# Decoder layers of a fused kernel: residual sums kept in PSUM, statistics of two blocks at once, the write-back moved, weights prepared in mid-slot

## The reference

```
x = x + attn(layernorm(x))          # 4 layers of width 128, hidden width 512
x = x + xattn(layernorm(x), ctx)    # channel selection by ctx (8 x 256 x 1024)
x = x + ffn(layernorm(x))           # top 2 of 8 experts, 1024 x 1024
```

```
h = x @ Win.T + bin
for each of 4 layers:
    y = silu(layernorm(h) )
    h = h + sconv(y) * scl              # decaying complex recurrence along the sequence
    y = silu(layernorm(h) @ W1.T + b1)
    h = h + y @ W2.T + b2
out = layernorm(h) @ Wout.T + bout

k = 154                                  # of 256 channels, for each of 1024 columns
mask = top_k(channel_map over channels, k)
```

## Time and profile before

| what | us |
|---|---|
| median of 3 runs (lowest, highest) | 1114.65 (1114.28, 1115.48) |
| the profiled execution: time, span | 1115.55, 1113.7 |
| busy over the span: PE, DVE, ACT, POOL | 1004.9, 555.0, 375.1, 447.8 |
| embedding and setup, until about | 99 |
| layer slots 0 to 16, until about | 371 |
| output product, mask applied, routing, until about | 592 |
| expert products, until about | 1101 |

### The profile page before, as it was taken

One profiled execution on the slowest core, in us unless ns is written; L12 is line 12 of the kernel. 1 busy time (PEld: TensorE's weight loads), 2 busy tenths in 40 slices (PEclk: granted clock), 3 DMA queues, 4 the chain that ended last, 5 costly groups with the idle time before them and its releaser, 6 DMA issues. The chain is left out here.

```text
span 1113.7 us, 13360 instructions
## 1 busy us (share of the span) xinstructions
PE 1004.9 (90%) x3534; PEld 531.0 (48%) x3535; DVE 555.0 (50%) x1660; ACT 375.1 (34%) x1016; POOL 447.8 (40%) x567
## 2 busy tenths in 40 slices
PE   5788889998998969799829999999999999999995
PEld 5687455564545435335514444444444444444442
DVE  5645779899997788978973111111111111111111
ACT  2334677786775328748820000000000000000000
POOL 3842455464653010008606433444333333333331
PEclk9878889999999989899958999999999999999998
DMA  7320111010000331003786473464637355373332
GB/s 300 119 92 3 49 49 38 30 67 1 1 1 1 152 114 39 1 1 155 296 322 232 89 227 79 128 182 129 176 76 229 77 138 163 75 226 75 75 76 38
DMA packets 38462, 120.25 MB, mean 108 GB/s; under 512 B 6220, under 2 KB 9351, under 8 KB 38408
## 3 DMA queue, kind: packets, MB, share of 16 engines
q1 hardware_dynamic: 25592, 79.77, 19.4%
q0 software_dynamic: 12816, 39.86, 16.4%
HBM read 82.91 MB, written 36.70 MB: 107 GB/s over the span
## 5 line engine op out<-in xcount | busy, mean ns | idle before, releaser
L2059 PE MATMUL bank<-T,X 128*128 x1184 | 508.4, 592 | 0.1
L2059 PEld LDWEIGHTS bank<-T,X 128*128 128x128 f32 x1184 | 224.9, 190 | 283.4 <-issue 283.4
L2121 DVE TENSOR_SCALAR X<-bank,col_p 128x512 f32<-128x512 f32 x37 | 27.8, 751 | 393.2 <-PE bank L2059 393.2
L2087 ACT ACTIVATE X<-bank,col_p 128x512 f32<-128x512 f32 x37 | 25.4, 688 | 495.1 <-PE bank L2059 467.0
L2010 POOL DMA_INDIRECT X<-x_nrm,col_s x156 | 150.4, 964 | 74.1 <-issue 47.2
L2019 POOL DMA_INDIRECT out_dram<-X,col_d x37 | 60.0, 1622 | 262.9 <-DVE X L2121 254.8
L479 POOL TENSOR_TENSOR rs<-ve,neg_half 128x4 f32<-128x4 f32 x36 | 37.5, 1041 | 114.7 <-DVE ve L960 114.7
L826 ACT ACTIVATE M<-X,T 128x256 bf16<-128x256 f32 x152 | 74.9, 495 | 2.0 <-POOLq L475 2.0
L645 PE MATMUL bank<-nat,T 128*128 128x512 f32 x128 | 64.0, 623 | 10.0 <-issue 7.4
L656 PE MATMUL bank<-X,T 128*128 128x512 f32 x128 | 62.5, 613 | 0.0
L2107 DVE STREAM_TRANSPOSE X<-X 128x1024 f32<-128x1024 f32 x39 | 48.4, 1240 | 27.4 <-DMA X<-x_nrm,col_s 16.9
(11 more groups left out here) (340 smaller groups left out, 1440.7 us busy)
## 6 DMA issues: line engine op xcount, KB each, us to landing
T<-in_L_ffn_expert_w_dram SPq DMA_DIRECT2D x8, 4096.0 KB, 17.6
out_dram<-X SPq DMA_DIRECT2D x17, 512.0 KB
M<-in_x_dram SPq DMA_DIRECT2D x16, 512.0 KB, 7.2
X<-in_x_dram SPq DMA_DIRECT2D x16, 512.0 KB, 6.6
x_nrm<-H SPq DMA_DIRECT2D x16, 512.0 KB, 3.0
T<-in_ctx_dram SPq DMA_DIRECT2D x9, 512.0 KB, 3.5
X<-x_nrm,col_s POOLq DMA_INDIRECT x156
X<-in_ctx_dram SPq DMA_DIRECT2D x4, 512.0 KB, 7.0
```

Source lines behind the costliest of these rows:

```text
L2059: mm = nc.tensor.matmul(bank[2 * u + n][:, :], xgt[u][:, k, :], Tf[:, ds(odd * D + (k * N + n * BANK), BANK)], start=(k == 0), stop=(k == ...
```

## The change

h of each chunk stays in a PSUM bank of its own (`HB`, banks 0 to 3) through all layers. In layer 0 `z(v)` puts H there by an identity matmul and adds the recurrence's product; later z(v) only adds, and `back(v)` adds to the same bank without an identity matmul. b2 is summed up over the layers beforehand, and ACT adds the sum so far when it reads the bank. `middle` moves from DVE to ACT (square from PSUM, then the copy to `H`), ahead of `hidden(s-1)` there. The variances go into the hidden banks 4 and 5, and both spreads into one bank 6, so new waits appear: `hidden(v)` waits in front of its second matmul for the plus-eps of visit v+3 (line 664 of the changed kernel), `var_first` and `var_second` for activations of the hidden layer, the spreads for scalings.

Statistics: one bn_stats call reads two column blocks alternately; it keeps even and odd elements apart, so its six results are count, mean and count times variance of each block. bn_aggr is gone, and the threshold constants absorb the square root of 256.

Order: on DVE plus-eps of s+2 comes first in the slot, `greatest(b7, h7, 0)` comes behind plus-eps of s. On ACT `last(s-1)` and the first copy come ahead of the second half of `count_second` and ahead of `count_last`. The steps of `prepare` for layers 1 to 3 come one slot later for PE, between `back(s-1, 0, 2)` and `var_second(s)`, and on DVE behind `turn_out(s+1)`.

```diff
-        PER_SIGN = math.sqrt(2 * math.pi) * math.exp(GUESS * GUESS / 2) / (2 * S)
+        PER_SIGN = math.sqrt(2 * math.pi) * math.exp(GUESS * GUESS / 2) / (2 * S) / math.sqrt(S)
+        GUESS /= math.sqrt(S)
...
-        BC1, BC2, ZB, OB, HD, SMALL, TURN = 0, 1, 2, 3, (4, 5), 6, 7
+        HB, BC, HD, TURN = (0, 1, 2, 3), 6, (4, 5), 7
...
-            at = (0 if first else 2 * TPC) + (v % 2) * TPC
-            return bank[SMALL][:, at:at + TPC]
+
+            return bank[HD[0] if not first else EARLY_VAR if v < 3 else HD[1]][:, 0:TPC]
...
+        def bias_so_far(v, out_):
+
+            layer = v // CH if out_ else v // CH - 1
+            return layer_par[:, layer, B2:B2 + 1] if layer >= 0 else 0.0
...
                 def var_second(v):
                     pe.wait_ge(sq2, v + 1)
-                    pe.wait_ge(ve1, v + 3)
+                    if v >= 1:
+                        pe.wait_ge(hid_act, (v - 1) * FT + 3)
...
                 def z(v):
...
-                    if v >= 1:
-                        pe.wait_ge(h_mid, v)
+                    if v >= CH:
+                        pe.wait_ge(h_out, v - CH + 1)
                     else:
+                        pe.wait_ge(emb_ev, v + 1)
+                        pe.wait_ge(ve1, 3 if v == 1 else 1)
                         pe.wait_ge(e_bcs, CH)
-                    nc.tensor.matmul(bank[ZB][:, :], cs[v // CH % 2], chunk(a_buf, v), start=True, stop=False)
+                        nc.tensor.matmul(h_bank(v), ident[:, :], chunk(H, v), start=True, stop=True)
+                    nc.tensor.matmul(h_bank(v), cs[v // CH % 2], chunk(a_buf, v), start=False, stop=False, skip_group_check=True)
...
                 def hidden(v):
...
+                        if t == 1:
+                            pe.wait_ge(ve1, v + 4)
...
                 def back(v, first, last):
...
-                        nc.tensor.matmul(bank[OB][:, :], ident[:, :], chunk(H, v), start=True, stop=False)
...
                         back(s - 1, 0, 2)
+                    for p, step in prepared(s - 1):
+                        if p > 0:
+                            prepare(p, step)
                     if 0 <= s < VISITS:
                         var_second(s)
...
+                def middle(v):
+                    act.wait_ge(z_mm, v + 1)
+                    a.activation(chunk(sq, v), h_bank(v), ACT.Square, bias=bias_so_far(v, False)).then_inc(sq2, 1)
+                    a.activation(chunk(H, v), h_bank(v), ACT.Identity, bias=bias_so_far(v, False)).then_inc(h_mid, 1)
...
-                def middle(v):
-                    dve.wait_ge(z_mm, v + 1)
-                    v_.tensor_tensor(chunk(H, v), chunk(H, v), bank[ZB][:, :], ALU.add).then_inc(h_mid, 1)
...
-                    for i in range(h * HT, (h + 1) * HT):
-                        v_.bn_stats(st_c[:, i, :], tile_y(b, i)).then_inc(c_stat, 1)
+                    for i in range(h * HT, (h + 1) * HT, 2):
+                        both = tile_y(b, slice(i, i + 2)).rearrange("p k s -> p s k")
+                        v_.bn_stats(st_c[:, i // 2, :, :].rearrange("p b c -> p (b c)"), both).then_inc(c_stat, 1)
```

More of the change, by code:

```diff
@@ L623, in spread_second @@
                     pe.wait_ge(rt2, v + 1)
-                    if v >= 1:
-                        pe.wait_ge(yn2, v)
-                    spread(v, BC2, bc2)
+                    pe.wait_ge(yn1, v + 3)
+                    spread(v, BC, bc2)
                 def z(v):
@@ L709, in embedded @@
                     for k in range(KD):
-                        mm = nc.tensor.matmul(bank[OB][:, u * P:(u + 1) * P], win_t[:, k, :], x_t[t % 2][:, k, :], start=(k == 0), stop=(k == KD - 1))
+                        mm = nc.tensor.matmul(bank[EMB][:, u * P:(u + 1) * P], win_t[:, k, :], x_t[t % 2][:, k, :], start=(k == 0), stop=(k == KD - 1))
                     mm.then_inc(emb_mm, 1)
@@ L721, in embed @@
                         pe.wait_ge(e_bcs, q)
-                    spread(q, ZB, e_bc)
+                    spread(q, EMB_BC, e_bc)
                 pe.wait_ge(const_ready, 10)
@@ L772, in _ @@
                     for p, step in prepared(s):
-                        if p == 0 or step < 2:
+                        if p == 0:
                             prepare(p, step)
@@ L891, in _ @@
                     if s == 0:
-                        act.wait_ge(h_mid, s + 1)
-                        square(s, sq2)
+                        middle(s)
                         silu(s + 2)
@@ L898, in _ @@
                         continue
+                    if 0 <= s < VISITS:
+                        middle(s)
                     if 0 <= s - 1 < VISITS:
                         hidden(s - 1)
-                    if 0 <= s < VISITS:
-                        act.wait_ge(h_mid, s + 1)
-                        square(s, sq2)
                     if starts(s, 6) is not None:
                         count_last(starts(s, 6), HT, KD)
+                    if starts(s, 3) is not None:
+                        count_first(starts(s, 3), 0, HT)
                     for p, step in prepared(s - 1):
@@ L908, in _ @@
                             prepare(p, step)
[L909 to L912, removed]
                     if 0 <= s + 2 < VISITS:
@@ L917, in _ @@
                     if starts(s, 4) is not None:
+                        count_second(starts(s, 4), 0, HT)
+                    if 0 <= s - 1 < VISITS:
+                        last(s - 1)
+                    if b0 is not None:
+                        copies(b0, 2 * h0)
+                    if starts(s, 4) is not None:
                         count_second(starts(s, 4), HT, KD)
@@ L920, in _ @@
                         count_last(starts(s, 5), 0, HT)
[L921 to L924, removed]
                     if b0 is not None:
@@ L1165, in _ @@
                         x_stats(s + 5)
+                    if 0 <= s + 2 < FINAL:
+                        plus_eps(s + 2, True, var1, ve1)
                     if 0 <= s + 1 < VISITS:
                         turn_in(s + 1)
-                    for p, step in prepared(s - 1):
-                        if p > 0 and step == 0:
-                            prepare(p, step)
                     if b7 is not None:
                         without_under(b7, h7)
-                    if 0 <= s < VISITS:
-                        middle(s)
-                    if 0 <= s + 2 < FINAL:
-                        plus_eps(s + 2, True, var1, ve1)
                     if b1 is not None:
                         stats(b1, h1)
-                        if h1 == 1:
-                            means(b1)
                     if 0 <= s + 1 < VISITS:
                         scan(s + 1)
+                    if 0 <= s + 2 < FINAL:
+                        scale(s + 2, h_out, s + 2 - CH + 1, bc1, yn1)
+                    if 0 <= s + 1 < VISITS:
+                        turn_out(s + 1)
+                    for p, step in prepared(s - 1):
+                        if p > 0 and step in (0, 2):
+                            prepare(p, step)
+                    if 0 <= s < VISITS:
+                        plus_eps(s, False, var2, ve2)
                     if b7 is not None:
                         greatest(b7, h7, 0)
-                    if 0 <= s + 2 < FINAL:
-                        scale(s + 2, BC1, bc1, yn1)
-                    if 0 <= s + 1 < VISITS:
-                        turn_out(s + 1)
-                    if 0 <= s < VISITS:
-                        plus_eps(s, False, var2, ve2)
                     if b9 is not None:
```

79 lines of the change are left out of this document (39 added, 40 removed).

## The result

The changed kernel takes **1123.49 us** (1122.64 to 1124.73, 4 runs); beside it the kernel before took 1114.47 (1113.99 to 1115.48). The ratio is 1.0078, 95% interval 1.0063 to 1.0093: **9.0 us slower**. I had forecast 1114.9, range 1103 to 1120, so it is outside. The profiled execution has a span of 1121.8.

The account below looks back on a forecast made before the run. Two loops within some tenths of each other bound the layers: DVE's own work and the chain through PE and DVE. Terms -3.0 + 0.4 + 0.4 + 2.4 = +0.2 us gave 1114.9 us, no change, range 1103 to 1120.

Parts of the forecast that it names:

- the loop: Layer slots: second scaling, hidden, spread, back, variance, eps, rest of DVE; 14.44 us without pick, 15.92 with.
- PE idles 0.8 to 2.5 ahead of each hidden: Layer slots: PE's wait before the hidden matmuls, listed among the signs that the forecast is right; no time charged.
- T to eps: Layer slots: from the start of hidden on PE to eps on DVE; 7.38 us without the identity matmul, 8.24 before.
- more clock lost in layer 0: First layer: the forecast's own way to come out measurably slower, with probability 0.09.
- greatest moved: DVE in layer slots: four MAX8 go from ahead of the first scaling to behind eps, adding 1.29 us there.
- the alternate read: DVE statistics: bn_stats of 512 over two blocks by turns takes 1.07 us, from the nearest stepped row.
- rival A: DVE statistics: the pair statistics run as adjacent ones, leaving 0.8 us of slack; 1112.8 us, chance 0.17.
- step 0: Weights on DVE: the first preparation step shows nearly in full, counted as 0.84 us a layer.
- rival C: DVE statistics: reading two blocks alternately is dearer than a step; 1119.6 us at 1.30 spacing, near 1134 at 2.0; chance 0.18.
- Weights in mid-slot: Weight preparation inside the slot: old waits of 0.78 and 1.80 go; 0.84, 0.97 and 0.81 us a layer are added.
- Layer 0: First layer: no saving, identity matmuls move into z and delay ACT's work; +2.4 us.
- Tail: End of channel selection: last visit loses 0.86 us of identity, but the MAX8 group comes 1.29 late; +0.4 us.

Follow-up runs that it names:

- keep_two: Changed kernel plus unread filler matmuls on PE ahead of hidden: two in slots 7, 9, 11, 13, 15, 16, one in the other slots 6 to 16; 1114.12 us.
- after_old_stats: Changed kernel with the old statistics (four bn_stats of 256 a slot, 8 aggregations in each second slot); 1121.47 us, ratio 1.0066 to the kernel before.
- greatest_early: Changed kernel with the first four MAX8 back ahead of the first scaling, nothing else; 1103.76 us, ratio 0.9893 to the kernel before.
- before_pair_stats: Kernel before with bn_stats over two blocks at once and no bn_aggr, nothing else; 1113.68 us, ratio 0.9991 to the kernel before.
- after_again: Changed kernel run once more, unedited; 1123.80 us, ratio 1.0080 to the kernel before.
- keep_one: Changed kernel plus one unread 512-column filler matmul on PE ahead of hidden in each of slots 6 to 16; 1117.14 us, ratio 1.0014 to the kernel before.

## Why the forecast was wrong

**What bounds the kernel, and the loop: right.** The two loops, 0.78 + 7.38 + 6.28 and 1.48 for `pick`, stand in the trace to 0.02 us where the clock is full and no weights are in the slot (slot 14: 15.91; keep_two's slots 9, 13, 15: 14.44, 14.43, 14.44). A layer came to 63.2 to 63.5 in keep_two, for 63.3; with its own clock the changed kernel has 66.34 and 68.29.

**The step that failed** is one clause: "PE idles 0.8 to 2.5 ahead of each hidden". I took it as a sign of a right loop, priced it at nothing, and put 7.38 for T to eps in every slot. It was too low, and it was not free. PE stood 1.97, 2.50, 1.97, 3.38, 3.36 and 3.43 us in slots 7, 9, 11, 13, 15 and 16, and hidden ran at half rate in each: 10.9 us, where the forecast had nothing; keep_two has them back. The sizes were in my own numbers: the MAX8 group's 1.29 behind eps, added to the waits before, gives 2.49 for slot 9, 3.25 for 13, 3.36 for 15 and 3.43 for 16. I had the clock in the text for layer 0 only, and a margin of 0.09 for "more clock lost in layer 0"; none of the rivals was this one. The Trainium skill (TensorE: Matmul & The Clock Gate, section "HAM oscillation — how this bites in real kernels") describes a loop of this kind, matmuls that wait in each turn and begin each turn slow; the rows here agree for six of the eleven slots from 6 to 16. The prediction does not weigh it for these slots.

**greatest moved: right in size, underrated in reach.** Each slot got its 1.29 behind eps (6.28 for 4.99). But I set it off against the identity product in one sum and did not see it as a choice: with it undone the same change takes 1103.8, 20 us less. By my count 8 of these are the clock (10.9 less the 2.9 still lost in slots 15 and 16), and the rest is shorter slots and tail. In the kernel before, the same move alone lengthened PE's waits as much and lost the clock too, with the identity product in place.

**Statistics: wrong value, right consequence.** I took 1.07 us for the alternate read, by the nearest stepped row; it is 0.69, rival A's condition and my own lower bound. The Trainium skill (Advanced Engine Details and Errata, section SBUF Cachelines) has a penalty for a new line at each access, and I held line 2131 to agree; this read, at 1 KB between the two blocks, shows none: 690 ns for 685. In the changed kernel DVE stood 0.65 to 2.11 us for the variance in every slot from 7 to 15 but 10, so a shorter instruction gained nothing there. In slots 6 and 10 it came late all the same, 9.04 after D, and step 0 cost 0.7 of the 0.84 forecast. That is luck: line 974, the turn out, took 1.51 and 1.50 there, for 0.68 in slot 5. With 0.68 DVE would have come at about 8.2, by these rows (an estimate), and step 0 would have cost next to nothing. What slows line 974 was not tested; POOL's line 498 ran beside it (206.17 to 207.44, line 974 from 206.48 to 207.99). The slower rival C had the right sign and the wrong mechanism: its alternate read was not dear at all.

**Weights in mid-slot: right in sum.** Over the plain loop keep_two's slots 6, 7 and 8 carry 0.71, 0.89 and 1.18 us, its slots 10, 11 and 12 0.72, 0.89 and 0.91: 2.8 and 2.5 a layer for the 2.62 forecast. The old waits of 0.78 and 1.80 are gone.

**Layer 0** came to +1.5 for +2.4, D of slot 1 to +3.0 for +3.2. That looks better than it is: after_old_stats shows that 3.2 us there hang on whether hidden in slot 1 runs at full or half rate after the same wait. **Tail**: +1.1 for +0.4; hidden of slot 16 at half rate is 1.4 of it.

**Open**: what past activity the clock goes by. No single wait orders the cases (the clock fell after 0.66 in one kernel and held after 3.53 in another), and I did not try to find it. Nor is it shown what part the missing identity product has in slots 15 and 16, where greatest_early lost the clock after the same waits that the kernel before stood at full rate: before_pair_stats lost it there too, with the product in place.

## What to carry to other kernels

Before counting a gain, add up how long PE will stand in each turn: work that another engine does behind its last wait is waiting for PE, once PE has run out of work of its own, and what PE does next may run at half rate. Here four MAX8 moved from ahead of a wait to behind it cost their length in each turn, lengthened PE's wait by as much, and cost more through the clock. If the wait must stay, PE can be given filler work there, sized to stay under the wait; a filler where there is no wait is a delay. Look at the granted clock of the stretch in each experiment before crediting a difference of a few us to the edit.

## What the runs showed of the hardware

- `bn_stats` over 512 elements of two blocks by turns (1 KB apart) takes 690 ns, over adjacent ones 685.
- Half rate of hidden followed waits from 0.66 to 3.53 us, and full rate followed waits of up to 3.53; two profiles of the changed kernel (after_again is the second) agreed in every slot.
- In slot 13, a wait of 1.55 for 2.41 (keep_two against keep_one, which has a filler of 0.86 us less there, and in slots 7, 9 and 11) took hidden from 5.37 to 3.94 us.
- In the layer slots of the changed kernel POOL's power for the first layernorm of a visit (line 490) took 1.38 to 1.96 us, that for the second 1.01 to 1.04; in the kernel before both took 1.01 to 1.04, but for two of 1.38 and 1.41. I did not test what slows it.
